# Graph layer over a dense 8192 × 8192 adjacency: every load issued by SyncE, cells cut by row quarters

## The reference

```python
h = jnp.maximum(_layernorm(x, axis=-1), 0.0)
A_hat = adj + jnp.eye(adj.shape[0])
d_inv_sqrt = jnp.sum(A_hat, axis=1) ** (-0.5)
A_norm = d_inv_sqrt[:, None] * A_hat * d_inv_sqrt[None, :]
out = x + jax.nn.relu(A_norm @ (h @ W.T))
```

## Time and profile before

| what | us |
|---|---|
| median of 3 runs | 1196.89 |
| lowest and highest | 1188.43, 1203.75 |
| the profiled execution, whole | 1185.19 |
| its span, first to last instruction | 1183.4 |

### The profile page before, as it was taken

One profiled execution on the slowest core, in us unless ns is written; L12 is line 12 of the kernel. 1 busy time (PEld: TensorE's weight loads), 2 busy tenths in 40 slices (PEclk: granted clock), 3 DMA queues, 4 the chain that ended last, 5 costly groups with the idle time before them and its releaser, 6 DMA issues.

```text
span 1183.4 us, 9349 instructions
## 1 busy us (share of the span) xinstructions
PE 949.1 (80%) x2363; PEld 434.0 (37%) x2363; DVE 838.8 (71%) x1081; ACT 553.6 (47%) x1655; POOL 128.8 (11%) x102
## 2 busy tenths in 40 slices
PE   1713053483768879899998999999999999899997
PEld 1511021131323334344443444444444444344443
DVE  7952043373656867788887888888888888787785
ACT  0766675667655755462735626226246272100011
POOL 4021020110210101010101010000010000010011
PEclk9966576786979899999999999999999999999999
DMA  9999999999899999999999999999999799999993
GB/s 336 370 400 344 364 389 335 320 319 359 300 365 366 339 350 347 306 367 343 328 332 336 337 316 368 342 270 314 309 264 287 205 330 287 281 274 322 337 337 94
DMA packets 260486, 381.33 MB, mean 322 GB/s; under 512 B 10449, under 2 KB 237905, under 8 KB 260433
## 3 DMA queue, kind: packets, MB, share of 16 engines
q1 hardware_dynamic: 130288, 190.40, 51.3%
q10 hardware_dynamic: 130144, 190.34, 50.6%
HBM read 376.50 MB, written 4.19 MB: 322 GB/s over the span
## 4 chain that ended last, share of the span: by engine, by line
PE 43%; ACT 3%; DMA 3%; ACTq 1%; DVE 1%; SPq 1%; issue 0%; POOLq 0%; POOL 0%; DVEq 0%
PE bank L508 42%; DMA slot<-in_adj_dram 3%; ACT junk L547 2%; ACTq L289 1%; ACTq L297 1%; DVE adjT L701 0%; PE pre L484 0%; ACT slot L537 0%; ACT kept_cell L565 0%; SPq L342 0%; SPq L335 0%; DVE kept_cell L787 0%; POOLq L190 0%; POOL kept_cell L439 0%; SPq L289 0%
## 5 line engine op out<-in xcount | busy, mean ns | idle before, releaser
L508 PE MATMUL bank<-adjT,support 128*128 128x512 f32 x2048 | 908.2, 605 | 177.8 <-DVE adjT L701 177.7
L508 PEld LDWEIGHTS bank<-adjT,support 128*128 128x128 f32 x2048 | 394.4, 194 | 669.6 <-issue 666.4
L701 DVE STREAM_TRANSPOSE adjT<-slot 128x1024 f32<-128x1024 f32 x430 | 526.5, 1237 | 108.6 <-PE bank L508 97.2
L547 ACT ACTIVATE junk<-slot 128x384 bf16<-128x384 f32 (+2 forms) x732 | 348.1, 477 | 256.6 <-issue 144.9
L537 ACT ACTIVATE slot<-slot 128x6144 f32<-128x6144 f32 (+11 forms) x56 | 166.4, 2971 | 158.8 <-issue 74.7
L685 DVE TENSOR_REDUCE part<-slot 128x4 f32<-128x1536 f32 (+2 forms) x61 | 95.2, 1562 | 133.1 <-DMA slot<-in_adj_dram 133.1
L547 ACT ACTIVATION_READ_ACCUMULATOR junk<-slot 128x1 f32 x732 | 136.5, 186 | 0.0
L701 DVE STREAM_TRANSPOSE adjT<-kept_cell 128x1024 f32<-128x1024 f32 x70 | 85.0, 1231 | 27.6 <-PE bank L508 27.6
L428 POOL COPY kept_cell<-slot 128x2048 f32<-128x2048 f32 x35 | 65.1, 1892 | 352.5 <-DVE adjT L701 352.5
L565 ACT ACTIVATE kept_cell<-kept_cell,dinv 128x128 f32<-128x128 f32 x64 | 20.2, 389 | 176.1 <-DVE adjT L701 86.7
L416 POOL TENSOR_TENSOR dinv<-total,power 128x4 f32<-128x4 f32 x16 | 16.1, 1007 | 477.5 <-DVE total L755 477.5
(11 more groups left out here) (53 smaller groups left out, 166.3 us busy)
## 6 DMA issues: line engine op xcount, KB each, us to landing
slot<-in_adj_dram ACTq DMA_DIRECT2D x134, 768.0 KB, 13.3
slot<-in_adj_dram SPq DMA_DIRECT2D x134, 768.0 KB, 14.5
slot<-in_adj_dram ACTq DMA_DIRECT2D x66, 512.0 KB, 11.7
slot<-in_adj_dram SPq DMA_DIRECT2D x66, 512.0 KB, 12.6
slot<-in_adj_dram ACTq DMA_DIRECT2D x8, 1536.0 KB, 20.6
slot<-in_adj_dram SPq DMA_DIRECT2D x8, 1536.0 KB, 21.2
slot<-in_adj_dram SPq DMA_DIRECT2D x4, 1408.0 KB, 14.3
slot<-in_adj_dram ACTq DMA_DIRECT2D x4, 1408.0 KB, 15.0
```

What stands on the lines that cost most here:

```text
L508: ins = nc.tensor.matmul(bank[bank_of(g)][:], support[:, v * R + t, :], adjT[at % TURNS][:, r, :], start=(n == first_of[g] and t == 0), st ...
L547: nc.scalar.activation(junk[at % JUNKS][:, :n], cells[:, c, :], ACT.Copy, accum_out=part[u % 2][:, k, c:c + 1]).then_inc(junk_done, 1)
L701: nc.vector.transpose(adjT[at % TURNS][:].rearrange("p t (c i) -> p t c i", i=Q), half.rearrange("p c (t r) -> p t c r", r=Q)).then_inc(t_ ...
```

## The change

The two patterns that cells and `x` are read by are turned round, SyncE takes over all loads but half of those of `x`, and ScalarE all stores:

```diff
-    adj_v = adj.rearrange("(bb u r) (b j) -> u b r bb j", bb=B, u=NB, b=B)
+    adj_v = adj.rearrange("(bb u r) (b j) -> u bb b r j", bb=B, u=NB, b=B)
-    x_runs = x.rearrange("(b u q c) f -> b q u (c f)", b=B, u=NB, q=Q)
+    x_runs = x.rearrange("(b u q c) f -> b u q (c f)", b=B, u=NB, q=Q)
...
-        def load_cells(queue, quarters, m):
+        def load_cells(m):
             kind, u, v, n = landing[m][:4]
-            for b in quarters:
-                queue.dma_start(piece(m)[b * Q:(b + 1) * Q, :, :],
-                                adj_v[u, b, :, :, v * CELL:(v + n) * CELL]).then_inc(ld_slot[slot_of[m]], 16)
-
-        def load_far(queue, quarters, m):
+            rows = piece(m).rearrange("p (c bb) j -> p bb c j", bb=B)
+            for bb in range(B):
+                nc.sync.dma_start(rows[:, bb, :, :],
+                                  adj_v[u, bb, :, :, v * CELL:(v + n) * CELL]).then_inc(ld_slot[slot_of[m]], 16)
+
+        def load_far(m):
             kind, u, bb, n, v, cells = landing[m]
             to = far_block(m).rearrange("p a (b j) -> p a b j", b=B)
-            b0 = quarters[0]
             for a in range(n):
-                queue.dma_start(to[:, a, b0:b0 + 2, :],
-                                adj_far[u, :, bb + a, b0:b0 + 2, v * CELL:(v + cells) * CELL]
-                                ).then_inc(ld_slot[slot_of[m]], 16)
+                nc.sync.dma_start(to[:, a, :, :], adj_far[u, :, bb + a, :, v * CELL:(v + cells) * CELL]
+                                  ).then_inc(ld_slot[slot_of[m]], 16)
...
-            if queue is nc.scalar:
-                queue.sem_inc(act_piece, 1)
-            else:
-                queue.wait_ge(act_piece, m + 1)
...
+        def load_x(queue, q):
+            for u in range(q * TX // R, (q + 1) * TX // R):
+                queue.dma_start(support[:, u * R:(u + 1) * R, :].rearrange("p c f -> p (c f)"), x_runs[:, u, :, :]).then_inc(ld_x[q], 16)
...
         def _(sp):
             sp.dma_start(w_sb[:], w).then_inc(ld_w, 16)
-            for q in range(XC):
-                for b in (0, 1):
-                    load_x(sp, b, q)
+            for q in range(0, XC, 2):
+                load_x(sp, q)
             for m in range(AGAIN):
-                load_piece(sp, (0, 1), m)
-            stored = 0
+                load_piece(m)
+            renewed = 2
             for m in range(AGAIN, len(landing)):
-                while stored < done_by(m):
-                    store(sp, (0, 1), stored)
-                    stored += 1
-                load_piece(sp, (0, 1), m)
+                while renewed < min(NB, 2 + done_by(m)):
+                    sp.wait_ge(o_ok, renewed - 1)
+                    load_xin(renewed)
+                    renewed += 1
+                load_piece(m)
...
             def far_sums(m):
                 u = landing[m][1]
                 act.wait_ge(ld_slot[slot_of[m]], landed[m])
-                next_piece(m)
...
+            for q in range(1, XC, 2):
+                load_x(act, q)
             act.wait_ge(ident_ok, 9)
...
+            for n in range(NB):
+                relu(n)
+                if n > 0:
+                    store(n - 1)
+            store(NB - 1)
```

More of the change, by code:

```diff
@@ L43, in gnn_kernel @@
     SLOTS = 4
-    AHEAD = 3
     HALVES = 2
@@ L127, in gnn_kernel @@
         before_in_slot.append(earlier[-1] if earlier else None)
-        landed.append(16 * sum(2 * landing[k][3] if landing[k][0] == "far" else B for k in earlier + [m]))
+        landed.append(16 * sum(landing[k][3] if landing[k][0] == "far" else B for k in earlier + [m]))
     by_act = [sum(landing[k][0] != "again" for k in range(m + 1)) for m in range(len(landing))]
@@ L283, in kept, with load_piece @@
             return kept_cell[:, 3]
-        def load_cells(queue, quarters, m):
+        def load_cells(m):
             kind, u, v, n = landing[m][:4]
-            for b in quarters:
-                queue.dma_start(piece(m)[b * Q:(b + 1) * Q, :, :],
-                                adj_v[u, b, :, :, v * CELL:(v + n) * CELL]).then_inc(ld_slot[slot_of[m]], 16)
-        def load_far(queue, quarters, m):
+            rows = piece(m).rearrange("p (c bb) j -> p bb c j", bb=B)
[3 more added lines that the diff above has]
+        def load_far(m):
             kind, u, bb, n, v, cells = landing[m]
             to = far_block(m).rearrange("p a (b j) -> p a b j", b=B)
-            b0 = quarters[0]
             for a in range(n):
-                queue.dma_start(to[:, a, b0:b0 + 2, :],
-                                adj_far[u, :, bb + a, b0:b0 + 2, v * CELL:(v + cells) * CELL]
-                                ).then_inc(ld_slot[slot_of[m]], 16)
+                nc.sync.dma_start(to[:, a, :, :], adj_far[u, :, bb + a, :, v * CELL:(v + cells) * CELL]
+                                  ).then_inc(ld_slot[slot_of[m]], 16)
         def transposed(n):
             return HALVES * (n + 1)
-        def load_piece(queue, quarters, m):
+        def load_piece(m):
             before = before_in_slot[m]
@@ L311, in load_piece @@
                 kind, u, v, n = landing[before][:4]
-                queue.wait_ge(t_done, transposed(place[u, v + n - 1]))
+                nc.sync.wait_ge(t_done, transposed(place[u, v + n - 1]))
             else:
-                queue.wait_ge(act_freed, by_act[before])
+                nc.sync.wait_ge(act_freed, by_act[before])
                 if landing[before][0] in ("left", "near"):
-                    queue.wait_ge(dve_freed, by_dve[before])
+                    nc.sync.wait_ge(dve_freed, by_dve[before])
@@ L317, in load_piece @@
                 if landing[before][0] == "near":
-                    queue.wait_ge(copied, landing[before][1] + 1)
-            if queue is nc.scalar:
-                queue.sem_inc(act_piece, 1)
-            else:
-                queue.wait_ge(act_piece, m + 1)
-            if landing[m][0] == "far":
-                load_far(queue, quarters, m)
-            else:
[L326 to L330, removed]
@@ L332, in load_xin @@
-        def load_xin(queue, quarters, n):
+                    nc.sync.wait_ge(copied, landing[before][1] + 1)
+            if landing[m][0] == "far":
+                load_far(m)
+            else:
+                load_cells(m)
+        def load_x(queue, q):
+            for u in range(q * TX // R, (q + 1) * TX // R):
+                queue.dma_start(support[:, u * R:(u + 1) * R, :].rearrange("p c f -> p (c f)"), x_runs[:, u, :, :]).then_inc(ld_x[q], 16)
+        def load_xin(n):
             u = finals[n]
-            for b in quarters:
-                queue.dma_start(xin[n % 2][b * Q:(b + 1) * Q, :, :],
-                                x_v[b, :, u * R:(u + 1) * R, :]).then_inc(ld_xin[n % 2], 16)
@@ L338, in store @@
-        def store(queue, quarters, n):
+            for b in range(B):
+                nc.sync.dma_start(xin[n % 2][b * Q:(b + 1) * Q, :, :],
+                                  x_v[b, :, u * R:(u + 1) * R, :]).then_inc(ld_xin[n % 2], 16)
+        def store(n):
             u = finals[n]
[L340 to L345, removed]
+            nc.scalar.wait_ge(o_ok, n + 1)
+            for b in range(B):
+                nc.scalar.dma_start(out_v[b, :, u * R:(u + 1) * R, :],
+                                    o[n % 2][b * Q:(b + 1) * Q, :, :]).then_inc(st_out[n % 2], 16)
@@ L358, in _ @@
             sp.dma_start(w_sb[:], w).then_inc(ld_w, 16)
-            for q in range(XC):
-                for b in (0, 1):
-                    load_x(sp, b, q)
+            for q in range(0, XC, 2):
+                load_x(sp, q)
             for m in range(AGAIN):
-                load_piece(sp, (0, 1), m)
-            stored = 0
+                load_piece(m)
+            renewed = 2
             for m in range(AGAIN, len(landing)):
-                while stored < done_by(m):
-                    store(sp, (0, 1), stored)
-                    stored += 1
-                load_piece(sp, (0, 1), m)
+                while renewed < min(NB, 2 + done_by(m)):
[3 more added lines that the diff above has]
+                load_piece(m)
                 if m == AGAIN + SLOTS:
                     sp.wait_ge(t_done, transposed(column_at[NB - 1] + BAND))
[L372 to L376, removed]
+                    load_xin(0)
+                    load_xin(1)
+            while renewed < NB:
+                sp.wait_ge(o_ok, renewed - 1)
+                load_xin(renewed)
+                renewed += 1
             for c in range(2):
```

6 lines of the change are left out of this document (1 added, 5 removed).

## The result

The changed kernel takes 3171.31 us, the median of 4 runs (3167.71 to 3174.74), beside 1195.38 us of the kernel before: a ratio of 2.652, 95% interval 2.634 to 2.670. Its profiled execution has a span of 3172.6 us. The forecast was 3360 us, within 3000 to 4000.

A forecast was written before the change was run, and what follows sets the result against it. Taken as bound by DMA, cells on four engines: cells 3027 + `x` 44 + far pieces 229 + `xin` and stores 30 + semaphores 6 = 3336 us; with start, end and time outside the span, 3360 us, range 3000 to 4000.

The forecast's parts named there:

- The shape sets the number of engines: Cell transfers: source outermost 4, destination 128, so each runs on the same four DMA engines, not 16; 0.85.
- The packet price: Time per packet on one DMA engine: 66.8 ns for 1536 bytes, 47.8 for 1024, 29.0 for 512.
- the first term: Cell pieces of 3 cells: 65 pieces, 33,280 packets on each of four engines at 66.8 ns, 2223 us.
- The line through the two prices: Packet time from the 6144-byte and 1536-byte prices: 10.2 ns + 0.0367 ns per byte.
- `x` on four engines: Loads of `x`, source outermost 4: 4.2 MB in 44 us, where it took a part of the first 15.
- Issuing: SyncE alone issues a cell piece in 2 to 4 us; not on the path while transfers bound, cost 0.
- TensorE: Matmuls under the transfers: 2048 × 0.75 = 1543 us even at low clock, under the 3300 of the four engines.
- The signs: If right: mean DMA share 0.31, about 113 GB/s; cell windows 0.25 at 92 GB/s; far windows still fast.
- Rivals 1 and 2: Spread over engines holds: 1, loads gain, 1130 us, chance 0.06; 2, nothing is gained, 1185 us, chance 0.04.
- rival 1: Cell transfers keep 16 engines and loads gain: first 560 us shorter by 55, 1130 us; chance 0.06.
- Rival 3: Cell transfers on four engines, each slower at 15.8 GB/s: 4650 us; chance 0.05.

The follow-up runs named there:

- e1: The changed kernel with cell pieces loaded by column quarters again (four transfers of 32 partitions), all still issued by SyncE: 1660.48 us, ratio 1.391.
- e2: The kernel before with cells alone changed to row quarters, two on SyncE's and two on ScalarE's queue: 3160.45 us, a single run.
- e3: The changed kernel with each cell transfer cut in two by pairs of column quarters, source outermost 2: 5910.97 us, a single run.
- e9: The changed kernel with cells 128 outermost on both sides (elements misplaced, only time counts) and `x` in its old shapes: 1153.23 us, ratio 0.971.
- e4: The kernel before with the loads of `x` alone in the new shape, source outermost 4, on both queues: 1239.24 us, ratio 1.041.
- e10: The kernel before with cells 128 outermost on both sides, two row quarters per queue (elements misplaced, only time counts): 1157.20 us, ratio 0.974.
- e6: The kernel before with column quarters dealt otherwise: SyncE loads 0, then 2, ScalarE 3, then 1; 1378.21 us, ratio 1.157.
- e7: The kernel before with far pieces whole on SyncE, ScalarE issuing only its half of cell pieces: 1240.26 us, ratio 1.044.
- e11: The kernel before with far pieces whole, in turn on SyncE and ScalarE, cells as before: 1208.51 us, ratio 1.016.

## Why the prediction was right

- *The shape sets the number of engines.* Right, and shown three ways: e1 takes the shape back and gives 1660 us; e2 puts it alone into the kernel before and gives 3160; e3 halves the outermost count and the rate halves (5911 us). e2 and e3 also show that it is always the same engines, for both queues and for every transfer: with others in turn the rates would have added up. (The views give shares of 16 engines' time, so "four engines" is read from a share of 26.6% and a rate that nothing raised.) What was an unseen mechanism in the prediction is measured here for outermost counts of 4 and 2. The rule of the Trainium skill's page "DMA: Bandwidth & Descriptors", section "Why a DMA increments its semaphore by 16 and not by 1", agrees: by it the engines are 4 and 2.
- *The packet price.* This is the term that was mis-sized. I took 66.8 ns for 1536 bytes from stretches with 16 engines at work and held it for the engine's own ("these rates are the engines' own"); four engines alone do it in 61.7 ns and two alone in about the same (25 GB/s each). That makes the first term 33,280 × 61.7 = 2053 us instead of 2223, 170 us of the 189 that the forecast is too high. The 1024-byte packets were cheaper too: the DMA view of 2240 to 2255 us of the kernel after shows

```profile
DMA packets 1427, 1.45 MB, mean 97 GB/s; under 512 B 12, under 2 KB 1427, under 8 KB 1427
```

  which is 1415 data packets, 42.4 ns each on four engines instead of 47.8, and 15,872 × 42.4 = 673 us instead of 759. These two corrections are 256 us, more than the 189, so other terms were dearer by some 70 us together. Some 26 us of them are holes between the first and the last piece, in which fewer than four packets were under way; where the rest lies isn't traced. The reason for the 5 ns is open: e9 has no crowding in one half of the partitions and is still at 373 GB/s, so most of it comes with 16 engines at once, wherever they meet. (The line through the two prices has 10.4 ns at its foot, not 10.2; this changes the sum by 3 us.)
- *`x` on four engines.* Right in kind: from 5 to 25 us of the kernel after, `x` alone ran at 102 GB/s. The sum put 44 us on the four engines for it. What it is worth there is not shown: e2, which loads `x` in the old shape, is only 11 us faster, and differs in more than `x`. In the kernel before it costs 45 us (e4).
- *Issuing.* Costed at 0, and right for this kernel: e2, with two queues and the handshake, is within 11 us of it. That SyncE issues with no trouble also holds at full rate, e9. What I had not foreseen is that the issue instruction is held while the engines are behind, so the chain names SyncE for 86%, and that in e4 this keeps far pieces from being issued.
- *TensorE.* The bound of 1543 us held: 1120.0 us for the matmuls of line 499, with 1902.0 us of waiting before them.
- *The signs.* A mean share of 0.31 and 113 GB/s were expected, 33.8% for both queues and 120 GB/s came; cell windows 0.25 at 92 expected, 0.266 at 100 measured; the far windows were as fast as before.
- *The rivals.* Rivals 1 and 2 needed 16 engines. e9 shows what they would have been: 1153 us, between 1130 and 1185. Of the gain of 55 us that rival 1 gave, 37 us were there (32 against the profiled execution, from which rival 1 counts). Rival 3 (four engines slowed further) is out: they were faster. The rule of the Trainium skill that the prediction cites for the change (page "DMA: Bandwidth & Descriptors", section "Rules for kernel authors": "Use one 128-partition transfer") held by 3% in e9 and e10, where both sides have 128 outermost, and not in the changed kernel, whose 128-partition transfers have a source with 4 outermost. That it matters which half of the partitions is written, 1.7 times in the rate, was not in the prediction, which had no row for it.

## What to carry to other kernels

Before a transfer is reshaped, write down the outermost dimension of both sides: the DMA engines at work were the largest number, up to 16, that cuts both (4 and 2 where the source had 4 and 2, 16 where both sides had a multiple of 16), and always the same ones, so a source of 4 × 128 rows runs on a quarter of the engines though it fills all 128 partitions. If a transfer covers 32 partitions, two queues have to be in different halves of the partitions, and to stay there; the plain way to keep that is a fixed half for each queue and equal bytes on both. Where the layout allows it, a transfer of all 128 partitions with 128 outermost on both sides doesn't need this care (e9, e10). When a chain names the issuing queue for most of the span, divide the time of an issue into the bytes of its transfer: if that is the rate of the window, the queue is only showing its backlog.

## What the runs showed that was not expected

- The same cells on the same 16 engines ran at 213 GB/s when all were writing into one half of the partitions (e1), and at 368 with two queues in different halves; in e6 the rate moves between these levels within microseconds.
- An issue on SyncE took 7.9 us, the time of its own 768 KB at 100 GB/s, once the engines were behind.
- An engine moved 1536-byte packets at 25 GB/s with four or two at work and at 23 with sixteen.
- Putting 1% of the bytes, `x`, on four engines at the start cost 4% (e4): both queues were held in issuing it for some 23 us, and the other twelve engines had next to nothing to do.
- Far pieces at 419 GB/s from one queue made the kernel 4% slower (e7); nearly two thirds of this went away when both queues carried the same bytes (e11).
